# A graph layer and a mixture of experts: the first expert layer of the closing visits computed by rows, copied and turned

## The reference

```python
x = x + _L0_gnn_ref(_layernorm(x, axis=-1), src, dst, edge_weight, W, b)
#     msgs = features[edge_src] * edge_weight[:, None]
#     agg  = segment_sum(msgs, edge_dst);  return agg @ W.T + b
x = x + _L0_ffn_ref(_layernorm(x, axis=-1)[None], gate_w, gate_b, w1, b1, w2, b2)[0]
#     idx  = argmax(softmax(x @ gate_w + gate_b))       # one expert of 8 per row
#     hmid = relu(einsum('ecd,edf->ecf', buf, w1) + b1) # 256 -> 1024
#     ybuf = einsum('ecf,efd->ecd', hmid, w2) + b2      # 1024 -> 256
#     y    = ybuf[idx, pos] * (prb * kept)              # at most 1563 rows per expert
```

## Time and profile before

| what | value |
|---|---|
| median of 3 runs | 2299.45 us (2298.04 to 2299.7) |
| profiled execution | 2296.34 us, span 2294.4 us |
| start of the first layer of visit 85, the first of the tail | 2129.8 us |
| PE busy / POOL busy / DVE busy / ACT busy in the span | 79% / 74% / 57% / 44% |
| instructions L1061 (visits 85 to 104) | 640 records, 74.8 us |
| instructions L1043 (visits 0 to 84) | 680 records, 359.2 us |

### The profile page before, as it was taken

The page is one execution under the profiler, slowest core; times in us unless marked ns, Lnnn a source line. Parts: engine busy times, 40 slices in busy tenths (PEclk is TensorE's granted clock), DMA queues, the critical chain, the costliest instruction groups (busy, mean ns, idle before and its releaser), DMA issues.

```text
span 2294.4 us, 38064 instructions
## 1 busy us (share of the span) xinstructions
PE 1823.2 (79%) x10160; PEld 1204.1 (52%) x10160; DVE 1296.4 (57%) x6670; ACT 1012.2 (44%) x2026; POOL 1696.9 (74%) x1774
## 2 busy tenths in 40 slices
PE   3444566767999988788888888888998998988899
PEld 1222234444667655554554555554565665665798
DVE  8877434445677655545545545555555655555453
ACT  6777423334555443434334334344443444444222
POOL 7777777777777777777777777777777777775465
PEclk9999976566999999999999898899999999998899
DMA  7766446667777776657667675756676676766468
GB/s 245 234 224 210 118 143 195 204 199 262 245 242 248 245 240 177 220 180 235 181 185 232 181 245 171 258 171 212 216 257 202 182 256 214 246 214 222 137 249 324
DMA packets 172813, 494.84 MB, mean 216 GB/s; under 512 B 48181, under 2 KB 86837, under 8 KB 149894
## 3 DMA queue, kind: packets, MB, share of 16 engines
q0 software_dynamic: 84960, 231.11, 34.1%
q1 hardware_dynamic: 70404, 235.95, 30.3%
q10 hardware_dynamic: 17234, 25.32, 3.1%
HBM read 596.46 MB, written 141.13 MB: 321 GB/s over the span
## 4 chain that ended last, share of the span: by engine, by line
POOL 50%; PE 20%; issue 17%; DMA 5%; DVE 4%; ACT 1%; SPq 1%; DVEq 0%; ACTq 0%; POOLq 0%
POOL msg L697 50%; PE ps L1073 6%; PE ps L1043 5%; DMA msg<-normed,src_sb 4%; PE ps L1061 3%; PE ps L951 2%; DMA hin<-rows_by_expert 1%; PE ps L960 1%; SPq L641 1%; ACT hmid L868 1%; DVE aggT L1288 1%; PE ps L1011 1%; DVE hmid L1431 0%; PE ps L1035 0%; PE ps L1052 0%
## 5 line engine op out<-in xcount | busy, mean ns | idle before, releaser
L697 POOL DMA_INDIRECT msg<-normed,src_sb x1457 | 1394.3, 957 | 443.9 <-issue 438.1
L951 PE MATMUL ps<-msg,onehot 128*32 128x256 f32 x3322 | 396.3, 470 | 191.2 <-DMA msg<-normed,src_sb 110.0
L1288 DVE TENSOR_TENSOR aggT<-aggT,ps 128x192 f32 x293 | 103.8, 354 | 603.2 <-PE ps L960 589.1
L1073 PE MATMUL ps<-wsl,hmid 128*128 128x256 f32 x1680 | 397.0, 390 | 4.6 <-ACT hmid L868 2.5
L1043 PE MATMUL ps<-wsl,hTf 128*128 128x512 f32 x680 | 359.2, 676 | 2.1 <-ACT hTf L858 1.7
L1073 PEld LDWEIGHTS ps<-wsl,hmid 128*128 128x128 f32 x1680 | 318.2, 195 | 59.3 <-issue 18.4
L820 ACT COPY pairs<-ps 128x256 f32<-128x256 f32 x293 | 108.7, 371 | 494.5 <-PE ps L951 483.8
L951 PEld LDWEIGHTS ps<-msg,onehot 128*32 128x32 f32 x3322 | 131.3, 122 | 347.8 <-DMA msg<-normed,src_sb 140.8
L960 PE MATMUL ps<-shift,pairs 128*128 128x96 f32 x1172 | 222.9, 321 | 102.8 <-ACT pairs L820 101.8
L960 PEld LDWEIGHTS ps<-shift,pairs 128*128 128x128 f32 x1172 | 189.3, 222 | 208.5 <-ACT pairs L820 175.4
L697 POOL DMA_INDIRECT msg<-in_x,src_sb x204 | 196.3, 962 | 64.4 <-issue 61.2
(11 more groups left out here) (148 smaller groups left out, 2535.1 us busy)
## 6 DMA issues: line engine op xcount, KB each, us to landing
wsl<-in_wsecond SPq DMA_DIRECT2D x105, 1152.0 KB
wsl<-in_wfirst SPq DMA_DIRECT2D x105, 1028.0 KB
rows_by_expert<-tiles_by_expert SPq DMA_DIRECT2D x752, 130.0 KB
msg<-normed,src_sb POOLq DMA_INDIRECT x1457
xrow<-in_x SPq DMA_DIRECT2D x97, 128.0 KB
wsl<-in_x SPq DMA_DIRECT2D x24, 512.0 KB, 4.2
normed<-wsl ACTq DMA_DIRECT2D x24, 512.0 KB, 3.1
tiles_by_expert<-srow ACTq DMA_DIRECT2D x94, 130.0 KB
```

What stands on the lines that cost most here:

```text
L697: pool.indirect_dma_start(out=msg[:, m + j, :], out_offset=None, in_=x if t < RAW else ln_dram, in_offset=bass.IndirectOffsetOnAxis(ap=src ...
L951: last = nc.tensor.matmul(ps[h * QWIN:(h + 1) * QWIN, t % 2, 0:D], onehot[:, j, :], msg[:, j, :], start=i == 0, stop=i == QUARTERS[q][h] - 1)
L1073: last = nc.tensor.matmul(ps[:, Y, 0:D], hmid[:, c, :], w2_at(v % 2)[:, c, :], start=c == 0, stop=c == FC - 1)
L1288: dve.tensor_tensor(columns, columns, ps[:, t % 2, D:D + KD * TWIN].rearrange("p (k c) -> p k c", k=KD), ALU.add).then_inc(s_added, 1)
```

## The change

The event `th` is put into the list for the tail's visits too, between `tf` of the next visit and `l2` of its own. Visit 84, whose `th` is written out by hand ahead of this part, is marked as done so that it doesn't get a second one. `TURNED` becomes 105. All twenty tail visits thereby take the form of L1043: rows held in PE, weights streamed 512 wide, two copies by ACT, eight turns by PE, and bias and relu moved behind these.

```diff
             elif queue:
                 for do in ("hl", "hn", "tf"):
                     once(do, queue[0][0])
+            if kind == "l2":
+                once("th", v)
             events.append((kind, v))
             if kind == "l2":
                 events.append(("z", v))
@@
     queue.pop(0)
     once("hl", queue[1][0])
     events.append(("pads",))
+    done.add(("th", first))
     planned = full
```

## The result

| | before | after |
|---|---|---|
| median | 2299.28 us (2298.04 to 2299.7, 4 runs) | 2340.73 us (2338.72 to 2343.56, 4 runs) |
| profiled execution, span | 2296.34, 2294.4 us | 2343.56, 2341.8 us |
| span up to the first layer of visit 85 | 2129.5 us | 2134.9 us |
| tail: from there to the end of the span | 164.9 us | 206.9 us |
| an undisturbed tail visit | 7.245 us | 9.317 us |

The account below looks back on a forecast made before the run. PE was taken to bound the tail, a visit's time being the sum of PE's work. Visits 88 to 104 add 34.9 us, visits 85 to 87 add 1.9, 3.9 and 2.4: 43.1 more, median 2342.5 us, range 2332 to 2356.

Parts of the forecast that it names:

- First layer: PE's first layer in a tail visit: 8 records instead of 32, 3.44 us instead of 3.57, so 0.13 less.
- Turns, bias and relu follow one another: Between a visit's layers: bias at 4.30, second layer at 5.77 instead of 3.79, a visit 9.30 us, 2.05 more.
- Undisturbed visits: Visits 88 to 104, without late row loads: each 2.05 us longer, 17 x 2.05 = 34.9 us.
- Plan ahead of the bias: DVE's plan, 1.94 us, now precedes its visit's bias: through at 3.15, no cost, except 1.9 us in visit 85.
- Visits 85 to 87: The tail's first three visits, where PE waits for DVE or row loads: 1.9, 3.9 and 2.4 us more.
- the step on the clock: Visit 86: a 4.2 us pause of PE lowers the clock, second layer 5.3 instead of 3.5, 1.8 us more.
- The clock as a rival for all visits: PE's 2.3 us between products lowers the clock in every visit: second layers 5.3 instead of 3.53, 2373 us; chance 0.07.
- PE's busy share in the undisturbed stretch: Sign in the profile after: PE's busy share there falls from 1.00 to about 0.87, at a clock of 1.00.
- the DMA share: Tail transfers: the same bytes in a longer visit, so the share falls from 0.81 to 0.63.
- PE's own work alone: Rival: bias and relu of half 0 stay hidden, a visit costs only 0.79 us more, 2321 us; chance 0.03.
- Weights as the pace of the tail: Rival: weight loads set a visit's 7.245 us and PE has slack, so 2297 us, not slower; chance 0.03.

Follow-up runs that it names:

- doubled turns: The changed kernel with each of the eight turns of a tail visit done twice: 2345.56 us, ratio 1.0186 to before.
- turns put first: The changed kernel with the hidden values turned ahead of the next visit's rows on PE, and relu ahead of those rows' copy on ACT: 2334.07 us.
- fused operation: The changed kernel with a tail visit's bias and relu in one ACT operation per block of 128, straight from PSUM, no DVE bias: 2320.66 us.
- moved plans: The kernel before with row loads of visits 87 and 88 issued earlier and DVE's plans of 89 and 90 behind visit 85's bias: 2290.14 us.

## Why the prediction was right

It was right in sign, size and mechanism: 2342.5 predicted (2332 to 2356), 2340.73 measured. Part of the closeness is luck, as errors in visits 85 to 87 cancelled in part. By its own steps:

- First layer, 0.13 less predicted: 3.43 against 3.57, so 0.14. Streaming 512 wide gains only this, since 8 records of 0.43 take nearly as long as 32 of 0.11.
- Turns, bias and relu follow one another, as the chain of waits shows: bias at 4.30 predicted, 4.28 found; second layer at 5.77 predicted, 5.78 found; from a waiting second layer to the next first layer 3.53 and 3.53. A visit was to take 9.30 and took 9.317. The doubled turns, the turns put first and the fused operation each moved this sum by what the path gives and not by PE's work.
- Undisturbed visits, 17 x 2.05 = 34.9: found 16 x 2.072 = 33.2 and 2.1 for the last, 35.3.
- Plan ahead of the bias, at no cost in an undisturbed visit: through at 2.96, right. In visit 85, where it should cost 1.9, the second layer starts 1.6 later (8.66 against 7.06).
- Visits 85 to 87, where the sum had 8.2 and the trace has 6.7 (2.7, 2.0, 2.0). Here the step on the clock was mis-sized twice. I put a fall of the clock, 1.8 us, on visit 86, with a pause of the products of 4.2 us; there it stayed at 1.00 (11.11 us, 2.0 more, the chain alone). And I put none on visit 85, where the second layer took 6.35 instead of 5.22, 1.1 more. The two errors cancel in part. Why the clock held in one pause and fell in the other isn't shown: both hold eight turns, and they are 4.15 and 5.25 us long. I had weighed the pauses by their length alone; visit 87 of the doubled turns shows that turns count too.
- The clock as a rival for all visits: it did not come about; 1.00 in 139.75 us. In visit 87 of the doubled turns the clock rose from 0.50 to 1.00 while PE had done nothing but turns since the first layer. The Trainium skill ("TensorE: Matmul & The Clock Gate", Part 4: PE-mode transpose), by which the full clock does not engage for turns, as they don't count as busy in the same way, is not borne out by that trace. The stretch at 0.50 from 2118.70, in which PE was busy mostly with turns, shows that not every stretch of them raises it.
- Two signs were missed in size. PE's busy share in the undisturbed stretch is 0.91 and not 0.87, and the DMA share 0.71 and not 0.63, though the rate fell as the longer visit asks. No run shows why the DMA engines were busy longer for the same bytes.
- PE's own work alone: refuted by the turns put first. Weights as the pace of the tail: refuted by the 2.07 us that each undisturbed visit got longer, and for the kernel before by the missing wait for `wsl`, though visits 86 to 88 come near it, as the moved plans show.

## What to carry to other kernels

Where one engine is busy all the time, look at what the old order lets the others do beside it before adding a hand-over between engines. Here eight turns cost 0.79 us of PE's work net by the prediction's rows, and 1.28 more came from waits between the engines, 0.86 of them PE's wait for the relu, which had lost its cover. What the form costs in visits 0 to 84, where other work of PE stands between turn and second layer, no run shows. If the form is wanted anyway, make the first dependent piece small: a bias and relu by blocks of 128, each with its own signal, gave back 0.88 of 2.07 us a visit here, and nothing in the form in which bias and relu were covered anyway.

A wait that ends at a load is worth following back to the load's place in its queue: two row loads of 130 KB, issued ahead of padding and weights, took 9.9 us out of the tail. Time won just ahead of a stretch that waits for loads came back as waits.

## What the runs showed of the hardware that I had not expected

- A granted clock that rises on turns alone: in visit 87 of the doubled turns it went from 0.50 to 1.00 between 2170.00 and 2170.20, where PE had done nothing but turns since the first layer ended, and the second layer took 3.53. In the same place with eight turns it stayed at 0.50, and the second layer took 5.31. More work of PE thereby left this visit 0.7 us shorter (16.6 and 17.3).
- Pauses of the products with eight turns in them: one of 4.15 us (visit 86 of the changed kernel) left the clock at 1.00; those of 5.2 to 5.4 us in visit 85 let it fall to a mean of 0.55 or 0.56 in the second layer, in all four kernels that had them.
- ACT's eight operations of bias and relu on 128 columns from PSUM took 2.19 us in all, 0.27 each, against 0.63 for a relu of 512 columns from SBUF; each is well within the 0.43 that PE needs for a block of the second layer (3.46 for eight).
- From one execution to the next, the part ahead of the tail varied by up to 13 us (2124.0 to 2136.8 in profiled executions of kernels that are the same there), while the undisturbed visits repeated to 0.01.
